# Layer-1 blocks of a two-layer transformer kernel: V as a tanh of ln Q, another order of the chunks, and operations over two chunks

## The reference

```
q, k, v = x @ Wq + bq, x @ Wk + bk, x @ Wv + bv
Q, K = elu(q) + 1, elu(k) + 1
KV   = sum over tokens of K * v          # one number per column
Ksum = sum over tokens of K              # one number per column
Z    = 1 / (Q * Ksum + 1e-6)
V    = Q * KV * Z
attn = gelu(V @ Wo + bo)
x    = layernorm(attn + x, ln1)
h    = gelu(x @ Wf1 + bf1)               # width 512
ff   = gelu(h @ Wf2 + bf2)
x    = layernorm(ff + x, ln2)
```

## Time and profile before

| | us |
|---|---|
| median of 3 runs (lowest to highest) | 2372.58 (2371.98 to 2374.55) |
| profiled execution, its own time | 2377.91 |
| its span in the trace | 2376.2 |
| busy in the span: PE, DVE, ACT, POOL | 1625.5, 1456.7, 1167.2, 418.5 |
| the eight blocks, from first product (1453.9) to last scale and bias (2063.6) | 610 |
| one block to the next (start of G2 of chunk 3) | 75.34 |

### The profile page before, as it was taken

One profiled execution on the slowest core, in us unless ns is written; L12 is line 12 of the kernel. 1 busy time (PEld: TensorE's weight loads), 2 busy tenths in 40 slices (PEclk: granted clock), 3 DMA queues, 4 the chain that ended last, 5 costly groups with the idle time before them and its releaser, 6 DMA issues.

```text
span 2376.2 us, 25413 instructions
## 1 busy us (share of the span) xinstructions
PE 1625.5 (68%) x9036; PEld 673.9 (28%) x9036; DVE 1456.7 (61%) x2635; ACT 1167.2 (49%) x2123; POOL 418.5 (18%) x374
## 2 busy tenths in 40 slices
PE   4000056133899999999984983877778677669998
PEld 2000045120222222222222431333333333334443
DVE  3999921747999999999903335545565555512222
ACT  3333200020788888888882336545565555412222
POOL 1477843420000000000000002110011100201111
PEclk7555555565899999999996996988899888879999
DMA  1000000025000000000011330000000000012240
GB/s 36 0 0 0 0 0 1 0 50 79 5 2 2 2 2 2 2 2 2 2 28 41 79 58 0 14 1 14 14 14 5 9 14 1 19 37 47 50 50 32
DMA packets 76085, 42.42 MB, mean 18 GB/s; under 512 B 21920, under 2 KB 72224, under 8 KB 75840
## 3 DMA queue, kind: packets, MB, share of 16 engines
q1 hardware_dynamic: 74576, 37.90, 8.2%
q10 hardware_dynamic: 1392, 3.02, 0.6%
HBM read 37.55 MB, written 3.15 MB: 17 GB/s over the span
## 4 chain that ended last, share of the span: by engine, by line
PE 41%; DVE 37%; ACT 9%; DMA 4%; issue 4%; POOL 3%; SPq 0%; ACTq 0%; DVEq 0%; POOLq 0%
DVE MX L744 14%; PE PS L799 5%; PE PS L1582 4%; PE PS L1583 3%; PE PS L1222 3%; PE PS L1592 3%; PE PS L821 3%; PE PS L440 3%; DVE ASPR L361 3%; DMA SB<-scr_w 3%; DVE N L1416 3%; ACT tmpb L865 2%; PE PS L1187 2%; PE PS L1202 2%; DVE ASPR L357 2%
## 5 line engine op out<-in xcount | busy, mean ns | idle before, releaser
L865 ACT ACTIVATE tmpb<-PS 128x512 f32<-128x512 f32 x1024 | 554.0, 595 | 144.6 <-PE PS L821 128.0
L744 DVE TENSOR_REDUCE MX<-PS 128x2 f32<-128x1024 f32 x512 | 585.3, 1215 | 56.9 <-PE PS L726 52.5
L799 PE MATMUL PS<-tmpb,VS 128*32 128x256 f32 x4096 | 324.6, 391 | 14.1 <-ACT tmpb L865 6.6
L726 PE MATMUL PS<-KST,QST 56*128 56x512 bf16 x1024 | 206.6, 401 | 66.0 <-DMA KST<-scr_k 37.7
L821 PE MATMUL PS<-QST,KST 59*128 59x512 bf16 x1024 | 200.5, 388 | 20.9 <-ACT tmpb L865 16.3
L1617 DVE TENSOR_TENSOR HG<-HG,PS 128x512 f32<-128x512 f32 (+1 forms) x96 | 65.9, 686 | 199.2 <-PE PS L1583 199.2
L424 PE MATMUL PS<-ident,QS 128*128 128x128 f32 x8 | 2.0, 428 | 244.9 <-DVE QS L370 244.9
L1607 ACT ACTIVATE HG<-PS 128x512 f32<-128x512 f32 (+1 forms) x96 | 57.2, 595 | 207.7 <-PE PS L1582 207.7
L379 ACT ACTIVATE ASPR<-S,SG 128x128 f32<-128x128 f32 x256 | 78.2, 388 | 138.0 <-POOL S L403 126.0
L1202 PE MATMUL PS<-X,WF 128*128 128x512 f32 x256 | 138.4, 681 | 6.9 <-ACT X L1327 6.9
L799 PEld LDWEIGHTS PS<-tmpb,VS 128*32 128x32 f32 x4096 | 82.3, 108 | 174.0 <-issue 80.6
(11 more groups left out here) (275 smaller groups left out, 2515.7 us busy)
## 6 DMA issues: line engine op xcount, KB each, us to landing
SB<-scr_w SPq DMA_DIRECT2D x16, 1024.0 KB, 14.6
WF<-in_L_attn_Wf SPq DMA_DIRECT2D x16, 256.0 KB, 3.0
QST<-NMP SPq DMA_DIRECT2D x192, 1.0 KB
...
```

The lines of the kernel that those rows point to most:

```text
L726: pe.matmul(PS[:, b + x, :], QST[r, 2 * g + jj, CH * qc + P * t:CH * qc + P * t + P], KST[r, g, cs(kc)], start=True, stop=True).then_inc(s ...
L744: r = v.tensor_reduce(MX[:, :, m // (TPC * NC), m // NC % TPC, m % NC], PS[:, b:b + 2, :], AX.X, ALU.max)
L799: last = pe.matmul(PS[32 * j:32 * j + 32, 3, h], VS[:, kt, u // NC, :], PB[:, kt % 2, j, h], start=(kt == 0 and half == 0), stop=(kt == NT ...
L865: a.activation(PB[:, kt % 2, j, :], PS[:, at % 3, :], ACT.Exp, scale=HD ** -0.5).then_inc(s_exp, 1)
```

## The change

V is written in another way. With a = Q Ksum, V = Q KV / (a + 1e-6) = (KV / Ksum) a / (a + 1e-6), and a / (a + 1e-6) = (1 + tanh((ln a - ln 1e-6) / 2)) / 2. So ACT takes Ln of Ksum Q (two operations over two chunks each), then Tanh (one a chunk, from the same table set as Gelu); the factor KV / (2 Ksum) goes into the rows of Wo (`WO2`), and the 1 of the bracket becomes a column (`WO2` times a vector of ones, one narrow matmul) that is added to `bo` (`GB`). KV is then needed for `WO2` alone, not for Ln. K is min(Exp, 1) + Relu in one DVE operation; Q is min(Exp, 1 + Relu) in two. K of chunks 1 and 2 (Exp, Relu, K, K times v) goes in operations over two chunks. Behind the last v product six products are issued into bank 7, which nobody reads. All four Wo products stand before F1(0), each into a bank of its own, and the order of the chunk work is another on each engine. The rest of the program differs only in three more constants that POOL sets at the start.

```diff
+        KBANK, VBANK, QBANK, OBANK = (1, 3, 4, 3), (5, 1, 2, 6), (0, 2, 0, 4), (7, 5, 3, 4)
         def pe_wo(pe, b, c):
-            n = NC * b + c
-            pe.wait_ge(s_vv, n + 1)
-            if n:
-                pe.wait_ge(s_g1, n)
-            pe.matmul(PS[:, 0, :], WA[:, b % 2, 3, :], Q1[:, cs(c)], start=True, stop=True).then_inc(s_wo, 1)
+            pe.wait_ge(s_vv, NC * b + c + 1)
+            pe.matmul(PS[:, OBANK[c], :], WO2[:, :], Q1[:, cs(c)], start=True, stop=True).then_inc(s_wo, 1)
...
+        def pe_body(pe, b):
+            n = NC * b
+            pe.wait_ge(s_wb, b + 1)
+            pe.wait_ge(s_qe, n + NC)
+            pe.matmul(PS[:, 0, 0:1], WO2[:, :], oneP[:, :], start=True, stop=True).then_inc(s_bm, 1)
+            pe_wo(pe, b, 0)
+            pe_wo(pe, b, 1)
+            pe_t1(pe, n)
+            pe_wo(pe, b, 2)
+            pe_wo(pe, b, 3)
+            pe_u1(pe, n)
+            pe_t1(pe, n + 1)
+            pe.wait_ge(s_g1, n + NC)
+            for m in range(NC):
+                pe_f1(pe, b, m)
+                if m < NC - 1:
+                    pe_f2(pe, b, m, range(KF))
+                    pe_u1(pe, n + m + 1)
+                    if m:
+                        pe_u2(pe, n + m - 1)
+                    if m + 2 < NC:
+                        pe_t1(pe, n + m + 2)
+                    elif b < NB - 1:
+                        pe.wait_ge(s_lw[(b + 1) % 2], LW * ((b + 1) // 2 + 1))
+                        pe_q(pe, b + 1, 0)
+                else:
+                    pe_f2(pe, b, m, range(KF // 2))
+                    pe_u2(pe, n + m - 1)
+                    pe_f2(pe, b, m, range(KF // 2, KF))
+                    if b < NB - 1:
+                        pe_k(pe, b + 1, 0)
+                pe_t2(pe, n + m)
...
+        def pe_inputs(pe, b):
+            n = NC * b
+            pe_q(pe, b, 1)
+            pe_k(pe, b, 1)
+            pe_k(pe, b, 2)
+            pe_v(pe, b, 0, *([(s_g2, n)] if b else []))
+            pe_q(pe, b, 2, (s_qe, n + 1))
+            if b:
+                pe_u2(pe, n - 1)
+            pe_v(pe, b, 1, (s_kr, n + 1))
+            pe_k(pe, b, 3, (s_kr, n + 3))
+            pe_q(pe, b, 3, (s_kr, n + 3))
+            pe_v(pe, b, 2, (s_qe, n + 2))
+            pe_v(pe, b, 3)
+            for _ in range(WARM):
+                pe.matmul(PS[:, 7, :], WA[:, b % 2, 0, :], HT[:, cs(0)], start=True, stop=True)
...
+        def act_inputs(a, chain, b):
+            a.preload_act_table_set("exp_and_others")
+            if b == 0:
+                act_qr(a, b, 0)
+            act_qe(a, b, 0).then_inc(s_qe, 1)
+            act_k(a, b, 0)
+            act_qe(a, b, 1)
+            act_qr(a, b, 1).then_inc(s_qe, 1)
+            act_k(a, b, 1)
+            if b:
+                act_x2(a, b - 1, NC - 1)
+            act_qe(a, b, 2)
+            act_k(a, b, 2)
+            act_qr(a, b, 2).then_inc(s_qe, 1)
+            act_qe(a, b, 3).then_inc(s_qe, 1)
             a.preload_act_table_set("natural_log")
             a.wait_ge(s_ks, b + 1)
-            for c in range(NC):
-                a.wait_ge(s_Q, NC * b + c + 1)
-                last = a.activation(ZR[:, c, :], Q1[:, cs(c)], ACT.Ln, scale=KS[:, 1:2], bias=eps1[:, 0:1])
+            for h in range(2):
+                a.wait_ge(s_p, n + 2 * h + 2)
+                c = slice(2 * CH * h, 2 * CH * h + 2 * CH)
+                last = a.activation(Q1[:, c], Q1[:, c], ACT.Ln, scale=KS[:, 1:2], bias=tiny1[:, 0:1])
             chain.link(last)
-            a.preload_act_table_set("exp_and_others")
-            for c in range(NC):
-                a.activation(ZR[:, c, :], ZR[:, c, :], ACT.Exp, scale=-1.0).then_inc(s_zr, 1)
             a.preload_act_table_set("gelu_apprx_tanh_and_others")
+        def act_v(a, b, c):
+            a.activation(Q1[:, cs(c)], Q1[:, cs(c)], ACT.Tanh, scale=0.5, bias=lnz1[:, 0:1]).then_inc(s_vv, 1)
...
+        def v_k(v, chain, b, g):
+            c = KGROUPS[g]
+            v.wait_ge(s_kr, NC * b + c.stop)
+            chain.link(v.scalar_tensor_tensor(out=RK[:, c, :], in0=EK[:, c, :], scalar=1.0, in1=RK[:, c, :],
+                                              op0=ALU.min, op1=ALU.add, accum_out=acc[:, 1, g:g + 1]))
...
+        def v_inputs(v, chain, b):
+            n = NC * b
+            if b:
+                v_stats(v, chain, 1, 6, s_t2, s_ep2, n - 1)
+            v_p(v, chain, b, 0)
+            if b:
+                v_apply(v, 1, 6, N2, s_r2, s_u2, s_n2, n - 1)
+            v_k(v, chain, b, 0)
+            v_p(v, chain, b, 1)
+            v_k(v, chain, b, 1)
+            v_kv(v, b, 0)
+            v_k(v, chain, b, 2)
+            v.tensor_reduce(KS[:, 1:2], acc[:, 1, :], AX.X, ALU.add).then_inc(s_ks, 1)
+            v_p(v, chain, b, 2)
+            v.wait_ge(s_qe, n + NC)
+            chain.link(v.tensor_scalar(ZR[:, 3, :], PS[:, QBANK[3], :], col(b, BQ), 0.0, ALU.add, ALU.max))
+            v_p(v, chain, b, 3)
+            v.wait_ge(s_ks, b + 1)
+            chain.link(v.tensor_scalar(KR[:, :], KS[:, 1:2], 1e-30, None, ALU.max))
+            v.reciprocal(KR[:, :], KR[:, :])
+            for g in (1, 2):
+                kv = v_kv(v, b, g)
+            chain.link(kv)
+            chain.link(v.tensor_reduce(KS[:, 0:1], acc[:, 0, :], AX.X, ALU.add))
+            chain.link(v.tensor_scalar(KG[:, :], KS[:, 0:1], KR[:, 0:1], 0.5, ALU.mult, ALU.mult))
+            v.tensor_scalar(WO2[:, :], WA[:, b % 2, 3, :], KG[:, 0:1], None, ALU.mult).then_inc(s_wb, 1)
+            v.wait_ge(s_bm, b + 1)
+            v.tensor_scalar(GB[:, :], PS[:, 0, 0:1], col(b, BO), None, ALU.add).then_inc(s_bo, 1)
```

More of the change, by code:

```diff
@@ L10 @@
+import math
 import struct
@@ L1191, in flat @@
             return N[:, :, :].rearrange("p t d -> p (t d)")
[L1193 to L1222, removed]
-                f.then_inc(s_f2, 1)
[L1224 to L1235, removed]
@@ L1245, in pe_blocks @@
         def pe_blocks(pe):
             pe.wait_ge(s_lw[0], LW)
[L1247 to L1251, removed]
-            for b in range(NB):
[L1253 to L1257, removed]
+            pe_q(pe, 0, 0)
@@ L1277, in act_q, with act_k @@
-        def act_q(a, b, c):
-            act_elu(a, b, c, QBANK[c], EQ, RQ, BQ, s_q, s_Q, s_qe)
-        def act_z(a, chain, b):
+        KGROUPS = (slice(0, 1), slice(1, 3), slice(3, 4))
+        def act_k(a, b, g):
+            c = KGROUPS[g]
+            n = c.stop - c.start
+            x = PS[:, KBANK[c.start]:KBANK[c.start] + n, :]
+            a.wait_ge(s_k, NC * b + c.stop)
+            a.activation(EK[:, c, :], x, ACT.Exp, bias=col(b, BK))
+            a.activation(RK[:, c, :], x, ACT.Relu, bias=col(b, BK)).then_inc(s_kr, n)
@@ new lines, in act_qe, with act_qr, act_x2 @@
+        def act_qe(a, b, c):
+            a.wait_ge(s_q, NC * b + c + 1)
+            return a.activation(Q1[:, cs(c)], PS[:, QBANK[c], :], ACT.Exp, bias=col(b, BQ))
+        def act_qr(a, b, c):
+            a.wait_ge(s_q, NC * b + c + 1)
+            return a.activation(ZR[:, c, :], PS[:, QBANK[c], :], ACT.Relu, bias=col(b, BQ))
+        def act_x2(a, b, c):
+            n = NC * b + c
+            a.wait_ge(s_u2, n + 1)
+            if b == NB - 1:
+                a.wait_ge(s_ga, 1)
+            a.activation(HT[:, cs(c)], PS[:, 7, :], ACT.Identity, scale=col(b, C2), bias=col(b, B2)).then_inc(s_bx2, 1)
@@ L1293, in act_g1, with act_x1 @@
+        def act_x1(a, b, c):
             n = NC * b + c
-            a.wait_ge(s_wo, n + 1)
-            if n:
-                a.wait_ge(s_y1, n)
-            a.activation(G1B[:, :], PS[:, 0, :], ACT.Gelu_apprx_tanh, bias=col(b, BO)).then_inc(s_g1, 1)
-        def act_slot(a, chain, b, t):
-            n, m, l = NC * b + t, NC * b + t - 1, NC * b + t - 2
-            first, middle, last = t < NC, 0 <= t - 1 < NC, t - 2 >= 0
-            tail = t == SLOTS - 1 and b < NB - 1
-            if middle:
+            a.wait_ge(s_u1, n + 1)
+            if n >= 2:
+                a.wait_ge(s_y2, n - 1)
+            a.activation(X1[:, n % 2, :], PS[:, 2, :], ACT.Identity, scale=col(b, C1), bias=col(b, B1)).then_inc(s_bx1, 1)
```

286 lines of the change are left out of this document (146 added, 140 removed).

## The result

The changed kernel took 2282.05 us (median of 4 runs, 2275.49 to 2285.68), the kernel before 2373.57 beside it: a ratio of 0.9602, with an interval of 0.9574 to 0.9630, and 91.5 us less. The forecast was 2278, in 2260 to 2302, and 95 us less.

What follows compares the result with a forecast made beforehand. No engine is full, so the order of waits bounds the kernel. Eight bodies -45.9, seven junctions -43.8 and block 0's inputs -5.4, clock loss included, sum to -95 from 2372.6: 2278 us, range 2260 to 2302.

Steps and rivals of the forecast that it cites:

- Body: Block part from first Wf1 product to second Gelu of chunk 3: 35.39 us at full clock instead of 42.83, 7.44 less.
- a chunk: One chunk's step in the block: 3.63 us from Wf1 to Wf2 plus 5.60 to the next Wf1, 9.23.
- F2 behind F1: On PE, Wf2 products follow Wf1 products directly, starting 3.63 us after them instead of 5.63.
- Junction: From second Gelu of chunk 3 to the next block's first Wf1 product: 26.25 us, 6.26 less than 32.51.
- the old block's x: Last x of the old block, which takes ACT from 6.95 us after the second Gelu of chunk 3.
- second Ln: Ln of the second half on ACT, starting 14.0 us after second Gelu of chunk 3, once DVE is done.
- Y1(0): Chunk 0's Y1 after Wo product and Gelu: 19.25 us after second Gelu of chunk 3, before 24.18.
- a doubled operation: Exp or Relu on ACT over 1024 columns, taken as 1.0 us each, between 0.58 and 1.16.
- Clock: PE clock falls about as the first Wf1 product starts in most blocks: 1.7 us a block, bounds 0 and 3.0.
- The clock holds: Rival: PE stays at full clock, all of 1.7 x 8 = 14 us is back, 2264; chance 0.15.
- The inputs take the place of the wait: Rival: in the junction V(0) must wait for DVE by 2 to 3 us a block, 2298; chance 0.2.
- The body stays at half clock: Rival: PE's level does not return within the body, a block about 96 us, 2535, slower; chance 0.03.

## Why the prediction was right

*Body.* Forecast 35.39 at full clock, measured 35.44; a chunk 9.23, measured 9.29, 9.22 and 9.23. That F2 behind F1 carries 3.2 us of it is shown by the experiment with transposes put between; of the 7.44 forecast, another 2.3 is the old half clock in F1(0), and 2 stay with the rest of the new order.

*Junction.* Forecast 26.25, measured 26.85. Up to Tanh every step lies within 0.2 us: the old block's x at 7.02 (forecast 6.95), second Ln at 14.14 (14.0), Tanh at 16.70 (16.5), Y1(0) at 19.36 (19.25). WO2 ends at 1529.28 and the first V at about 1529.65, so KV was off the way, by a third of a microsecond. The step that was off is "at full clock its short steps take half, which I estimate at 1.3": from Y1(0) to F1(0) it is 7.49 (1539.14 - 1531.65), 0.84 less than the old 8.33, not 1.3. POOL, DVE and ACT have most of that chain, and I had no row for the transposes alone at both levels. Two slips in the working did little: Y1(0) at 19.25 does not follow from 17.3 + 1.07 + 0.72, which is 19.1, and the 1.0 us of a doubled operation is a distance from start to start (measured 1.00, 1518.15 - 1517.15), while the 1.13 set beside it is a length (measured 1.14), so the "0.1 us dearer" compares two things.

*Clock.* Forecast 1.7 a block in most blocks. The price was right (1.69: 5.55 against 3.86 for F1(0), the same in the period), the count was not: four blocks of eight, 6.8 us instead of 13.6. The sum hid it, since the junctions cost 0.6 x 7 = 4.2 more and block 0 won 4.7 (its F1 at 1475.16 - 1447.75 = 27.4 behind the last x, before 32.1) instead of 5.4. And I had taken the first old period, 75.34, for all seven; their mean is 75.16, which takes away 1.3. Forecast -95, measured -95.7 between the two profiles: the agreement to a microsecond is luck, errors that met.

*Rivals.* "The clock holds" was half true in this kernel, and true with three more idle products. Had the level fallen in all eight blocks, as I thought, the time would have been some 7 us longer. "The inputs take the place of the wait": it turned out as 0.16 us a block in which ACT waits for DVE. "The body stays at half clock" did not happen. On the slower side I had looked at the wrong place: the way to a slower kernel from here was an order in which one engine's list is ahead of the others', 111 us by the experiment with F2 behind F1.

*What is settled, and what stays open.* A block won 12.2 us: 5.7 in the junction and some 6.5 in the body. Undone alone, F2 behind F1 costs 3.5 a block (3.2 without the clock), V 1.9, the idle products 1.8, the joined operations 0.5 without the clock. These do not add up to 12.2 and need not: the rest is shorter K and Q on DVE, Relu moved across, the four Wo products in a row, k and q begun in the body, and the half clock in F1(0) (2.3 in every block before, 1.7 in every second now), none of which was tried alone. When exactly the level falls is left open; it was seen between 1.5 us (the old kernel with idle products) and 5 us (the changed one without) behind PE's last dense work, and in half of the cases not at all.
